# Attention kernel with a mixture-of-experts layer behind it: VectorE's three jobs of a quarter turn in another order

## The reference

```
q, k, v = heads(norm(x) @ Wq.T), heads(norm(x) @ Wk.T), heads(norm(x) @ Wv.T)
a = q @ k.T * 512**-0.5 + (adj + adj)          # per head, rows that are all 0 give 0
x = x + (softmax(a) @ v) @ Wo.T
s = max(norm(x) @ gate_W + gate_b, 1e-4); p = softmax(s); top 2 experts, weights max(p, 0.1), scaled to sum 1
x = x + sum over the 2 experts of weight * (norm(x) @ expert_W[e] + expert_b[e]) / 2
```

## Time and profile before

| what | value |
|---|---|
| median of 3 runs | 1660.67 us (1660.43 to 1661.73) |
| the profiled execution's own time | 1662.81 us |
| its span | 1661.0 us |
| mean granted clock of PE | 0.970 |
| busy: PE, DVE, ACT, POOL | 1550.8, 1215.8, 955.9, 974.0 us |

### The profile page before, as it was taken

How to read it: one execution, slowest core, us unless ns; L and a number is a source line. 1 busy time by engine, 2 the same in 40 slices (tenths; PEclk the granted TensorE clock), 3 DMA queues, 4 the chain that set the end, 5 groups by cost and what they waited for, 6 DMA issues and landing times. The chain is left out here.

```text
span 1661.0 us, 45460 instructions
## 1 busy us (share of the span) xinstructions
PE 1550.8 (93%) x12808; PEld 1410.9 (85%) x12808; DVE 1215.8 (73%) x4952; ACT 955.9 (58%) x3129; POOL 974.0 (59%) x1788
## 2 busy tenths in 40 slices
PE   6999999999999999999999999966189999999996
PEld 6999999999999999999999999955167777777775
DVE  5578888888888888888888788877745555555554
ACT  4687777777777777777777777775111111111111
POOL 3255666566666666566665666556235565565655
PEclk9999999999999999999999999977599999999998
DMA  6787988789888888888887888794658898898886
GB/s 226 194 233 199 257 241 241 237 248 253 246 241 240 244 247 239 237 239 247 228 244 225 246 233 228 221 293 142 217 102 158 168 174 164 162 169 165 164 160 106
DMA packets 188629, 351.98 MB, mean 212 GB/s; under 512 B 20960, under 2 KB 30304, under 8 KB 188256
## 3 DMA queue, kind: packets, MB, share of 16 engines
q1 hardware_dynamic: 135520, 238.47, 51.7%
q0 software_dynamic: 29680, 69.55, 21.6%
q10 hardware_dynamic: 23184, 41.05, 8.0%
HBM read 189.48 MB, written 159.52 MB: 210 GB/s over the span
## 5 line engine op out<-in xcount | busy, mean ns | idle before, releaser
L678 ACT ACTIVATE prob<-prob,nmax 128x128 f32<-128x128 f32 x1024 | 398.8, 395 | 175.3 <-DVE amax L833 168.8
L1146 POOL TENSOR_TENSOR prob<-prob,rinv 128x512 f32<-128x512 f32 x256 | 261.4, 1042 | 241.3 <-DVE rinv L850 241.2
L829 DVE CUSTOM_DVE_ANT_0 prob<-ps_s,bias 128x128 f32<-128x128 f32 x1024 | 237.7, 287 | 142.1 <-PE ps_s L530 106.5
L1343 POOL DMA_INDIRECT out<-yt,token x135 | 211.6, 1567 | 196.3 <-DMA out<-yt,token 72.3
L1281 ACT ACTIVATE xgT_hi<-ps_x 128x512 fp32r<-128x512 f32 x135 | 80.7, 598 | 386.8 <-PE ps_x L1266 339.4
L1260 PE MATMUL ps_y<-we,xgT_hi 128*128 x540 | 260.8, 483 | 5.8 <-DVE xgT_lo L1300 5.8
L1261 PE MATMUL ps_y<-we,xgT_hi 128*128 x540 | 214.8, 398 | 0.0
L1262 PE MATMUL ps_y<-we,xgT_lo 128*128 x540 | 214.0, 396 | 0.0
L678 ACT ACTIVATION_READ_ACCUMULATOR prob<-prob,nmax 128x1 f32 x1024 | 196.7, 192 | 0.0
L833 DVE TENSOR_REDUCE amax<-prob 128x4 f32<-128x512 f32 x256 | 175.6, 686 | 8.9
L539 PE MATMUL ps_t<-const,prob 128*128 128x128 f32 x1024 | 164.8, 284 | 15.2 <-ACT pT L716 12.1
(11 more groups left out here) (191 smaller groups left out, 4770.4 us busy)
## 6 DMA issues: line engine op xcount, KB each, us to landing
ks<-kq_parts SPq DMA_DIRECT2D x192, 256.0 KB, 4.2
qs<-kq_parts SPq DMA_DIRECT2D x192, 256.0 KB, 6.3
xg<-x_lists ACTq DMA_DIRECT2D x135, 260.5 KB
xin<-x SPq DMA_DIRECT2D x64, 256.0 KB, 7.2
kq_parts<-kT_hi SPq DMA_DIRECT2D x32, 512.0 KB, 3.8
kq_parts<-kT_lo SPq DMA_DIRECT2D x32, 512.0 KB, 4.8
kq_parts<-qT_hi SPq DMA_DIRECT2D x32, 512.0 KB
kq_parts<-qT_lo SPq DMA_DIRECT2D x32, 512.0 KB
```

The lines of the kernel that those rows point to most:

```text
L678: last = nc.scalar.activation(prob[:, r, c, h, :], prob[:, r, c, h, :], ACT.Exp, bias=nmax[:, r, i:i + 1], scale=-1.0, accum_out=rsum[:, r ...
L829: last = nc.vector.tensor_tensor_reduce(out=prob[:, r, c, h, :], in0=ps_s[c % 2][:, P * h:P * h + P], in1=bias[:, b % 4, :], scale=-1.0, s ...
L1146: tt(prob[:, r, q], prob[:, r, q], rinv[:, r, HC * q:HC * q + HC].unsqueeze(2).to_broadcast([P, HC, P]), ALU.mult)\
L1343: pool.indirect_dma_start(out=out, out_offset=bass.IndirectOffsetOnAxis(ap=token[:, m, :], axis=0), in_=yt[:, r, :], in_offset=None, compu ...
```

## The change

Inside a quarter DVE now does `residual` first (where the quarter has it), then `low_part`, and only then `attention_max`. `inverse_sums` and everything behind it stay where they were. The same instructions are issued in the same number; no other engine's program changes.

```diff
                 for c in range(DC):
-                    if ok(t):
-                        attention_max(t, c)
+
+                    if odd and c == 1 and ok(t - 3):
+                        residual(t - 3)
+                    if odd and c == 3 and ok(t - 2):
+                        residual(t - 2)
                     if c:
                         low_part(t, c - 1)
                     else:
                         low_part(t - 1, DC - 1)
+                    if ok(t):
+                        attention_max(t, c)
                     if c == 0 and ok(t - 1):
                         inverse_sums(t - 1, 1)
                     if c == 2 and ok(t):
                         inverse_sums(t, 0)
                     low_part_of_x(t, c)
-                    if odd and c == 1 and ok(t - 3):
-                        residual(t - 3)
-                    if odd and c == 3 and ok(t - 2):
-                        residual(t - 2)
```

## The result

The changed kernel takes 1803.11 us (median of 4 runs, 1799.09 to 1806.22), the kernel before 1660.55 us beside it. The ratio is 1.0843, 95% interval 1.0828 to 1.0859. Forecast were 1794 us and a range of 1720 to 1880 us. The profiled execution of the changed kernel took 1799.1 us, the shortest of the four, its span 1797.3 us at a mean granted clock of 0.950. The span before was 1661.0 us, so 136.3 us have come in.

The account below looks back on a forecast made before the run. PE sets the pace before; after the change DVE and ACT do. New waits of 7.62 us less 3.11 us of old ones, net 4.51 us a pair, add 133 us: 1794 us, range 1720 to 1880 us.

Parts of the forecast that it names:

- The chain and its links: Maxima, exponentials, high part, low part, next maxima form one chain between DVE and ACT; one link is 3.87 us.
- E0: Quarter 0 of a pair's even turn: DVE ready after 3.91 us, high part there after 4.67 us, wait 0.76 us.
- E1: Quarter 1 of the even turn: DVE ready after 1.98 us, high part after 3.87 us, wait 1.89 us.
- O2: Quarter 2 of the odd turn: DVE ready after 1.57 us, high part after 3.87 us, wait 2.30 us.
- E2: Quarter 2 of the even turn: `weigh` and `find_places` lie between, 5.80 us against 3.87 us, no low-part wait.
- The residual's wait for O: In quarter 1 of the odd turn the residual waits for the previous quarter's projection O: 2.67 us.
- VectorE's slack: DVE's pair of 34.09 us less its waits for others leaves a 31.0 us sequence, so 3.1 us of slack.
- The clock: Rival: PE's idle time makes the clock fall in each pair, 47 us more, 1841 us; chance 0.15.
- TensorE's idle time: In E2 PE's right half waits for the first step of `find_places`, idle for about 3.2 us.
- Faster: Rival: the even turn's last V projection gets its bank early, PE stays the bound, 1650 us; chance 0.05.
- no difference: Rival: the new waits just fill DVE's slack, 1661 us; chance 0.04.
- O1 does not wait for O: Rival: PE is not held at the even turn's last V projection, the 2.67 us go, 1715 us; chance 0.13.

Follow-up runs that it names:

- longer_link_after: Changed kernel with one extra ScalarE copy to a spare tile right before each high part of K and Q: 1868.74 us, ratio to before 1.1265.
- longer_link_before: Kernel before with the same extra ScalarE copy to a spare tile before each high part of K and Q: 1663.54 us, ratio 1.0014.
- weigh_later_after: Changed kernel with the weights of the experts (`weigh`) moved one quarter later, behind the maxima: 1753.76 us, ratio 1.0538.
- low_first: Kernel before with only the low parts moved ahead of the maxima, the residual staying behind them: 1719.67 us, ratio 1.0335.
- o1_residual_back: Changed kernel with the `c == 1` residual put back behind the maxima, the other residual and low parts left in front: 1748.33 us, ratio 1.0505.

## Why the prediction was right

- **The chain and its links.** Right. The waits in E0, E1 and O2 were put at 0.76, 1.89 and 2.30 us, and are 0.93, 1.89 and 2.20 us; in E2 there is none. The hand-over from ScalarE to a waiting VectorE, taken as 0.05 us, is 651.93 - 651.32 - 0.57 = 0.04 us. `longer_link_after` against `longer_link_before` shows that the chain is closed in the one kernel and open in the other.
- **The residual's wait for O.** Right in its path, as `weigh_later_after` and the wait for `gate_x` show; put at 2.67 us, it is 1.75 us in the timeline and 2.0 us on average. Another 0.45 us or so stand before the low part of the transposed rows (L815), between the maxima of E2 and the residual, and I had not named them. Together 2.2 to 2.4 us.
- **VectorE's slack.** The step "DVE has only 3.1 us of slack in a pair" was wrong as an idea: `low_first` lost 1.9 us a pair to 2.4 us of waits. Most of those 3.1 us were already the end of a path from the maxima of E2 through two other engines. In the sum this did no harm, because the full change counts that same path, with its residual, as the new wait: 4.51 us net a pair, 4.62 us measured in an undisturbed one.
- **Sizes that cancelled.** From E1 to E2 VectorE needed 0.59 us less than the 6.47 us of the earlier trace rows: 0.44 us are the operation at L929, and most of the rest is the wait of 0.21 us before the maxima there, which the low part now covers. From O2 to O3 the links of the prediction give 4.15 - 0.21 - 0.67 + 1.90 = 5.17 us, and it took 5.75 us; 0.5 us of that are the operation at L893 (last section for both). That one makes up for the other is luck. And the sum took off 2.90 us for the old wait, an average over all pairs; its own links, added up as starts, give 38.80 us, not 38.6.
- **The clock.** The forecast's sum leaves it out, and the prediction named a clock that falls regularly as a sign of being wrong. That sign came. In stretches of 4 us the clock read below 0.99 in 20 of the 27 pairs, in one to three stretches each, down to 0.50; in the kernel before, no such stretch lies between the earlier trace rows and turn 60. The forecast held because the falls were cheap. All pairs together are 8 us longer than 27 x 38.71 us, not 47 us, and of the 13 undisturbed pairs nine had a fall. Of these 8 us some 6 lie from O2 to O3, 5.97 us on average against 5.75, where the gate's operations were stretched beside GpSimd in six pairs. The rule of the Trainium skill ("TensorE: Matmul & The Clock Gate", "HAM oscillation — how this bites in real kernels") agrees with the trace in that the clock fell in 20 of 27 rounds, and not in the cost: 8 us in 136. Of the 20 falls 18 begin in TensorE's E1 and two in E2, and TensorE had waiting time in E2. That this is why they are cheap is read from the trace; no run isolates it.
- **TensorE's idle time.** It idled in E2, as put, but 1.70 us and not 3.2; it idled 2.22 us in E1, where I had put nothing. There it waits for ScalarE's copy of the transposed probabilities, which stands behind the delayed high part of K.
- **The partial pairs** were put at 11 us, and are 7 us.
- **The rivals.** "Faster" and "no difference" hung on the new waits staying under a slack. `low_first` shows that this is not enough: its 2.4 us of new waits are under the 3.1 us and still cost 1.9 us a pair. "O1 does not wait for O" is what `weigh_later_after` made, by another edit. It gave 1754 us and not the rival's 1715 us, since VectorE's own work then took nearly the place of the wait.

The two halves do not add: 2.5 us for the one, 57 us for the other, 143 us together. With the low parts behind the maxima, the residuals in front cost nearly nothing. With the low parts in front, they cost 2.75 us a pair (38.71 against 35.96 us), and putting one or the other back gives 1.93 or 0.87 us, 2.80 us together. In O1 the residual is free once it fills VectorE's wait for the high part of K.

## What to carry to other kernels

Where two engines hand work to each other in fixed order, write down for each step which of its inputs the other engine makes behind something that itself waits for this engine. Here such a step, the low part, was free behind the one that feeds the other engine and cost 57 us by itself ahead of it. An engine's idle time before a wait is slack only if the thing waited for does not hang on the engine's own earlier work; follow it back once around the loop before counting on it. And a step moved later has consumers at the end of other queues: of the two gains tried here one shrank from 12 us to 3 and the other became a loss of 24 us there.

## What the runs showed of the hardware

Operations of 8 or 16 elements on VectorE with both inputs in SBUF took about 0.2 us or up to 1.1 us, and the long ones all ended with an operation of GpSimd. By line, 100 to 1080 us, before and then changed (count, busy us, mean ns):

```profile
L929 DVE TENSOR_TENSOR em<-eexp,mask 128x16 f32<-128x16 f32 x28 | 16.8, 601 | 0.0
...
L893 DVE TENSOR_TENSOR dlt<-score,m 128x16 f32<-128x16 f32 x28 | 4.9, 175 | 1.0
```

```profile
L929 DVE TENSOR_TENSOR em<-eexp,mask 128x16 f32<-128x16 f32 x24 | 4.0, 165 | 0.0
...
L893 DVE TENSOR_TENSOR dlt<-score,m 128x16 f32<-128x16 f32 x24 | 15.8, 659 | 0.8
```

The two operations have changed roles. In the kernel before all 28 at L929 begin inside GpSimd's subtraction for the low part of the attention result and end within 0.04 us of its end; none of those at L893 begins inside such an operation. In the changed kernel 20 of 24 at L893 do, inside the scaling of the probabilities, and none at L929. One of the 20 ends at 655.68 + 0.72 = 656.40 us, where the first of the two GpSimd operations, 1.02 us each, ends at about 656.4 us:

```profile
655.68 0.72 DVE L893 TENSOR_TENSOR dlt<-score,m 128x16 f32<-128x16 f32 x1
```

```profile
655.33 2.04 POOL L1147 TENSOR_TENSOR prob<-prob,rinv 128x512 f32<-128x512 f32 x2
```

In `longer_link_after` it was L892 (the second step of the gate's scores, L888 in the other two kernels), with 974 ns a time against 239 ns in the kernel before and 289 ns in the changed one. In `o1_residual_back` and `weigh_later_after` L893 takes 207 and 176 ns; that is the 0.5 us which they gained beyond what was expected. The Trainium skill, "GPSIMD Engine Reference", section "Specifications", names the SBUF interface as shared with VectorE, with contention for VectorE instructions that have two SBUF inputs. The traces agree: L888, L893 and L929 have two such inputs, and the minima with one input from PSUM take 286 ns beside GpSimd and away from it. Not every operation of GpSimd did this: in the kernel before, 49 operations at L888 that begin inside its power operation on 128x1, 0.57 us long, took 223 ns. So the price of such an operation is a matter of where it lands, about 0.5 us here, and it moved the sum by that much in each of two places. No run varied it alone.
